# Layer weights loaded into tiles shared with the attention, and the attention's last projections and the layer switch re-placed, in an adaLN transformer block on one core

## The reference, cut to what matters

```python
h = _layernorm(x) * (1 + ca) + sa
x = x + ga * _L0_attn_ref(h, ...)                # 4 heads, all 1024 keys, rms-normed q and k
h = _layernorm(x) * (1 + cb) + sb
x = x + gb * _L0_ffn_ref(h, ...)

def _layer(x, wqkv, qs, ksc, wo, lg, lb, w1, b1, w2, b2):       # twice
    h = shift_token(x)                           # the second half of the features comes from the token before
    q, k, v = jnp.split(h @ wqkv, 3, axis=-1)    # 256 -> 3 * 512
    q, k = rotary_xpos(l2norm(q) * qs, l2norm(k) * ksc)
    x = x + local_attention(q, k, v) @ wo
    h = _layernorm(shift_token(x)) * lg + lb
    a, g = jnp.split(h @ w1 + b1, 2, axis=-1)    # 256 -> 2 * 682
    return x + (a * gelu(g)) @ w2 + b2
```

## Time and profile before

| | us |
|---|---|
| median of 3 runs | 2210.22 (2209.44 to 2210.82) |
| profiled execution | 2207.61 |
| its span | 2205.8 |

### The profile page before, as it was taken

How to read it: one execution, slowest core, us unless ns; L and a number is a source line. 1 busy time by engine, 2 the same in 40 slices (tenths; PEclk the granted TensorE clock), 3 DMA queues, 4 the chain that set the end, 5 groups by cost and what they waited for, 6 DMA issues and landing times.

```text
span 2205.8 us, 36469 instructions
## 1 busy us (share of the span) xinstructions
PE 1865.4 (85%) x12941; PEld 1403.2 (64%) x12941; DVE 1510.0 (68%) x3723; ACT 1186.2 (54%) x2717; POOL 996.6 (45%) x788
## 2 busy tenths in 40 slices
PE   5569999999954799888899888987888999888986
PEld 3444444444433587776777867766776777777776
DVE  3678878877653685766867758584776857768673
ACT  0545545443433656656566565664656566565562
POOL 0325544647463444444444435543545445454451
PEclk7779999999976999999999999998999999999998
DMA  4000010101024000000000002011000000000000
GB/s 141 24 26 27 1 34 11 41 16 51 15 67 134 11 20 17 19 12 24 20 17 21 10 26 68 17 53 32 25 16 29 27 26 25 18 30 26 26 18 22
DMA packets 83407, 68.58 MB, mean 31 GB/s; under 512 B 10853, under 2 KB 79509, under 8 KB 83225
## 3 DMA queue, kind: packets, MB, share of 16 engines
q1 hardware_dynamic: 83224, 66.25, 9.7%
HBM read 45.22 MB, written 16.81 MB: 28 GB/s over the span
## 4 chain that ended last, share of the span: by engine, by line
PE 35%; DVE 18%; issue 6%; ACT 5%; DMA 2%; SPq 1%; POOL 1%; DVEq 0%; ACTq 0%; POOLq 0%
PE bank_O L1201 4%; PE bank_T L1189 3%; PE bank_A L260 3%; PE bank_A L262 3%; PE bank_P L260 3%; PE bank_A L261 3%; ACT l_sm L1337 3%; PE bank_P L261 2%; PE bank_P L262 2%; DVE l_t L1512 2%; PE bank_A L1178 2%; DVE l_sm L1528 2%; DVE l_u_lo L1594 2%; PE bank_T L1168 2%; PE bank_T L260 1%
## 5 line engine op out<-in xcount | busy, mean ns | idle before, releaser
L1737 POOL TENSOR_TENSOR l_sm<-l_sm,l_rinv 128x512 f32<-128x512 f32 (+1 forms) x256 | 250.1, 998 | 366.1 <-DVE l_rinv L1536 365.8
L1725 POOL TENSOR_TENSOR l_t<-l_qk,l_tab 128x512 f32<-128x512 f32 x128 | 170.1, 1350 | 328.8 <-DVE l_ss L1495 328.8
L1337 ACT ACTIVATE l_sm<-l_sm,l_nb 128x256 f32<-128x256 f32 (+1 forms) x512 | 248.1, 486 | 82.0 <-DVE l_nb L1528 81.8
L260 PE MATMUL bank_A<-l_f_hi,l_w_hi 128*114 128x256 f32 (+1 forms) x768 | 220.1, 287 | 3.7 <-DVE l_f_lo L1573 2.7
L262 PE MATMUL bank_A<-l_f_hi,l_w_lo 128*114 128x256 f32 (+1 forms) x768 | 216.0, 281 | 0.0
L261 PE MATMUL bank_A<-l_f_lo,l_w_hi 128*114 128x256 f32 (+1 forms) x768 | 215.8, 281 | 0.0
L1528 DVE CUSTOM_DVE_ANT_0 l_sm<-bank_A,l_mask 128x256 f32<-128x256 f32 (+1 forms) x512 | 177.1, 401 | 52.0 <-PE bank_A L1178 51.5
L1189 PE MATMUL bank_T<-ident,l_sm 128*128 128x128 f32 x960 | 149.1, 290 | 65.7 <-POOL l_sm L1737 34.4
L618 ACT ACTIVATE pr<-ps_S 128x1024 f32<-128x1024 f32 x128 | 130.7, 1023 | 125.4 <-PE ps_S L512 124.6
L1594 DVE TENSOR_TENSOR l_u_lo<-l_up,l_u_hi 114x256 fp32r<-114x256 f32 (+1 forms) x192 | 197.8, 1036 | 0.1
L861 POOL TENSOR_TENSOR acc<-acc,pr 128x1024 f32<-128x1024 f32 x64 | 155.8, 2435 | 51.0 <-ACT pr L618 46.5
(11 more groups left out here) (268 smaller groups left out, 5127.3 us busy)
## 6 DMA issues: line engine op xcount, KB each, us to landing
l_xs<-x_layers SPq DMA_DIRECT2D x64, 128.0 KB, 2.5
x<-in_x SPq DMA_DIRECT2D x8, 512.0 KB, 3.9
base_rows<-x SPq DMA_DIRECT2D x16, 256.0 KB, 2.1
x_layers<-x SPq DMA_DIRECT2D x16, 256.0 KB, 2.1
l_xs<-x_layers SPq DMA_DIRECT2D x64, 64.0 KB, 2.2
x_layers<-l_yb SPq DMA_DIRECT2D x32, 128.0 KB, 1.8
l_base<-base_rows SPq DMA_DIRECT2D x32, 128.0 KB, 3.1
out<-l_yb SPq DMA_DIRECT2D x32, 128.0 KB, 1.7
```

Source lines behind the costliest of these rows:

```text
L260: pe.matmul(out, a_hi, b_hi, start=(start and k == 0), stop=False)
L1337: eng.activation(row, row, ACT.Exp, bias=nb[:, R % SS, e:e + 1], scale=-1.0, accum_out=rsum[:, R % SS, e:e + 1]).then_inc(ex_ready, 1)
L1725: eng.tensor_tensor(dst[:, :, :, lo:lo + H2], src[:, :, :, hi:hi + H2], table[:, :, 1, lo:lo + H2].unsqueeze(2).to_broadcast([P, 2, LH, H2 ...
L1737: eng.tensor_tensor(row, row, rinv[:, R % SS, :].unsqueeze(2).to_broadcast([P, 2, P * windows(n)]), ALU.mult).then_inc(pn_ready, 1)
```

## The change

Five tiles (x, qk, scr, m1, x2) are allocated once for both blocks. The attention uses them as before, and the layers put their own tiles into them (`layer_tiles`). Around this:

1. In the attention, at tick (10, 8), SP issues the loads of the first layer's wqkv, w2 and wo, of the mask, of b2 and of the gains (`load_layers`, 13 DMAs), after waits for the last readers of these tiles. At the layers' start only load(0), load(1), the table, load(2), load(3) and w1 are left to SP.
2. The last two projections go to the banks S0 and S1 instead of X; DVE takes the last reciprocals and `normalise` before the projections' eviction, and `y_split` before the row statistics.
3. DVE modulates the last four row pairs, 12 to 15.
4. SP doesn't wait for the stores at the attention's end; a load of layer 1 waits for the h0 stores of its own sequence, and w1's loads for all stores.
5. In g = -1, first_w2_wo goes from POOL to DVE (k = 4), norms(0) from k = 8 to 6, rotated(0) from 9 to 7, rotated(1) to 9; the table is multiplied in four parts; trig(1) and trig(3) wait until DVE's norms are done; trig(3) goes to round 2 of group 0, and v of units 2 and 3 to its rounds 0 and 2.
6. In group 7, wqkv's pieces go one to a round, at 5 to 10, DVE subtracts them, and the table's parts stand at rounds 8 to 11. In group 8, wo goes to round 4, w1 to 5, 9 and 10, w2 to the slots k = 7, 9 and 11 through other buffers. The waits of later steps for these are narrowed. The gains of layer 2 are loaded in group 1.

The diff, cut to its core:

```diff
+def layer_tiles(share):
+    x, qk, scr, m1, x2 = (share[n] for n in ("x", "qk", "scr", "m1", "x2"))
+    at = {"qk": qk[:, 0:3 * 2 * LH * HD].rearrange("p (i h d) -> p i h d", i=3, h=2 * LH),
+          "pt": qk[:, 3 * 2 * LH * HD:16 * D].rearrange("p (i c n) -> p i c n", i=2, c=4),
+          "sm": x[:, 0:SS * 4 * P].rearrange("p (i e n) -> p i e n", i=SS, e=2),
...
@@ attention_block
         def h0_last(i):
-            return i in (4 * B - 3, 4 * B - 1)
+            return i >= 4 * (B - 1)
...
-                    at = "X"
+                    at = "X" if kind != "w" or i < 4 * B - 2 else f"S{i % 2}0"
...
+                last = R - A_LAG == A_RUNS - 1
+                if last:
+                    inverse(A_UNITS - 1, 0), inverse(A_UNITS - 1, 1)
+                    normalise(A_UNITS - 1)
                 for kind, i in fills(n, j):
                     evict(kind, i)
...
+            def load_layers():
+                t.wait_ge(done["qt"], 4 * A_HALVES)
+                t.wait_ge(done["xt"], 2 * A_HALVES)
+                t.wait_ge(h1_ready, 4 * A_HALVES)
+                t.wait_ge(scr_used, 6 * A_HALVES)
+                at = layer_tiles(share)
+                eng.dma_start(at["raw_q"], io["wqkv"][0].rearrange("(k p) n -> p k n", k=KC)).then_inc(early["wq"], 16)
...
+                load_scales(eng, io, at["scales"], early["tab"], 0)
...
+                if n == A_HALVES + 2 and j == 8:
+                    load_layers()
...
-            for f in range(4):
-                t.wait_ge(base_stored[f], 16 * B)
-                t.wait_ge(h0_stored[f], 16 * B)
@@ layers_block
+        LATE_V = ((2, 2), (3, 2))
-        W_Q = {2: (0, 1), 3: (2, 3), 8: (4, 5)}
-        W_O = {2: (0, 1)}
-        W_1 = {3: (0, 1), 7: (2, 3), 8: (4, 5)}
+        W_Q = {5: (0,), 6: (1,), 7: (2,), 8: (3,), 9: (4,), 10: (5,)}
+        W_O = {4: (0, 1)}
+        W_1 = {5: (0, 1), 9: (2, 3), 10: (4, 5)}
...
-        AT_O, AT_1, AT_2 = pieces[0:2], pieces[2:4] + pieces, pieces[0:2] + pieces[3:4]
+        AT_O, AT_1 = pieces[0:2], pieces[2:4] + pieces
+        AT_2 = [pt[:, i, :, :].rearrange("p c n -> p (c n)") for i in range(2)] + pieces[3:4]
...
@@ PE
+                        elif r in (0, 2):
+                            qkv(*LATE_V[r // 2])
@@ ACT
-                        if g == GL and k == 0:
-                            piece_2(0), piece_2(1), piece_2(2)
+                        if g == GL and k in (7, 9, 11):
+                            piece_2((k - 7) // 2)
@@ DVE
             def layer_norm(q, scale):
                 if q >= (UL - QUAD) // 2:
-                    w.wait_ge(wq_ready, KC + 6)
+                    w.wait_ge(wq_ready, KC + 3)
...
+                        if g == GL - 1:
+                            for i in W_Q.get(r - 1, ()):
+                                piece_q(i)
...
-                    if g == -1 and k == 7:
-                        first_w1()
+                    if g == -1:
+                        if k == 4:
+                            first_w2_wo()
+                        if k == 6:
+                            norms(0)
+                        if k in (7, 9):
+                            rotated(k // 8)
+                        if k == 7:
+                            first_w1()
@@ POOL
+                if n in (1, 3):
+                    w.wait_ge(chain, norms_done[n // 2])
...
-            tables(0)
+            for i in range(4):
+                tables(0, i)
...
+                        if r == 2 and g == 0:
+                            trig(3)
...
-                            for i in W_Q.get(r, ()):
-                                piece_q(i)
-                            if r == 10:
-                                tables(1)
+                            if r >= 8:
+                                tables(1, r - 8)
...
-                    if g == GL and k == 0:
-                        piece_2(0), piece_2(1), piece_2(2)
+                    if g == GL and k in (7, 9, 11):
+                        piece_2((k - 7) // 2)
...
-                    if g == -1 and k == 5:
-                        first_w2_wo()
@@ SP
+                else:
+                    for f in range(4):
+                        w.wait_ge(early["h0"][f], 16 * (b + 1))
...
             load(0), load(1)
-            eng.dma_start(raw_q, io["wqkv"][0].rearrange("(k p) n -> p k n", k=KC)).then_inc(wq_loaded, 16)
-            load(2), load(3)
-            tables(0)
...
+            table(), load(2), load(3)
+            for f in range(4):
+                w.wait_ge(early["base"][f], 16 * B)
+                w.wait_ge(early["h0"][f], 16 * B)
...
                     w.wait_ge(trig_ready, 3 * UL)
-                    tables(1)
+                    table()
                 if g == GL:
                     take_rest()
+                if g == 1:
+                    w.wait_ge(tab_ready, 4)
+                    load_scales(eng, io, scales, tab_loaded, 1)
...
+                if g == GL:
+                    take_2(0)
                 shift(first + 3)
+                if g == GL:
+                    take_2(1), take_2(2)
```

184 lines of the change are left out of this document (98 added, 86 removed).

## The result

| | before | changed |
|---|---|---|
| median of 4 runs, us | 2209.83 (2204.66 to 2210.82) | 2188.27 (2183.93 to 2189.37) |
| profiled execution, us | 2207.61 | 2188.08 |
| its span, us | 2205.8 | 2186.3 |

The ratio is 0.9902, with a 95% interval of 0.9885 to 0.992: 21.6 us faster. The forecast was 2174 in a range of 2160 to 2190. The direction is right and the time lies in the range, but outside the narrower 2163 to 2185 that the prediction gave the forecast itself: 36.5 us were forecast and 60% of them came. The question is where the other 15 went.

The account below looks back on a forecast made before the run. TensorE, busy 85% of the span, was taken as the bound, so only its standstills or half-clock stretches could give time: seam -23, group 7 0, group 8 -13.5, sum -36.5 from 2210.2, forecast 2174 us, range 2160 to 2190.

Parts of the forecast that it names:

- The seam up to the first matmul: From the attention's last projections to the layers' first matmul: earlier projections, modulation, load(0) and weights, -16.0 us.
- ScalarE's wait of 7.78: At the layers' start: ScalarE's wait for w2 and wo goes, -7.8 us.
- part A: The seam, from the attention's last projections to group 0's first probabilities: -23 us, bounds -29 to -18.
- The term of +3.1: At the layers' start: VectorE's three subtractions of w2 and wo, 2.9 us and a bit more beside GpSimd.
- The first rival: Seam and group 7: moved subtractions stand fully behind GpSimd instructions, 2182 us in all, chance 0.12.
- trig(3)'s -5.0: Norms' chain ahead of group 0 freed of trig(3), -5.0 us; trig(3) inside group 0 costs +1.75.
- Group 7: Second layer's wqkv and table loads: the wait for the table offsets the gain, 0 us, bounds -6 to +4.
- Group 8: Second layer's wo, w1 and w2 loads, excess 17.3 us: -13.5 us, bounds -16 to -9.
- the 13.0 go: In group 8, the 13.0 us of excess behind the second residual vanish; 4.3 arise in the rounds before it.
- The prediction's own sign of being wrong: Group 8 keeping more than 9 us of its excess would mean the stop was not w2's.
- the third rival: Layers' start: w1's loads, cast and subtractions or TensorE's low clock give back half of part A, 2188 to 2190, chance 0.03.
- the rival of dearer tile addresses: All 16 groups: shared tiles at other SBUF addresses make operations dearer, kernel slower, 2215 us, chance 0.02.

Follow-up runs that it names:

- e9: Kernel before the change, with only w2's DMAs of both layers cut into 112 rows and the rest, and their wait counts adjusted: 2192.2 us, ratio 0.9928.
- e8: Changed kernel with the early loads undone, the old DMAs back at the layers' start in the old order: one run of 2198.58 us.
- e1: Changed kernel with the second layer's w2 DMAs cut into 112 rows and the rest: 2180.55 us, ratio 0.986.
- e6: Changed kernel with the three subtractions of w2 and wo back on GpSimd, behind trig(0): one run of 2187.8 us.
- e3: Changed kernel with trig(3) back behind trig(2), without the wait for the norms' chain: one run of 2185.54 us.
- e4: Changed kernel with w2's and wo's casts and subtractions moved to the layers' very start, behind the first two units' inputs: 2184.46 us, ratio 0.9872.
- e5: e4 with w1's casts and subtractions also moved behind the fourth unit's input: 2177.44 us, ratio 0.986.
- e11: e10 with trig(3) back behind trig(2), without the wait for the norms' chain: 2164.21 us, ratio 0.9798.
- e10: Changed kernel with e2, e5 and e7 together: 2166.28 us, ratio 0.9806.
- e2: Changed kernel with the table's DMA in group 7 issued ahead of wqkv's last two pieces: 2181.92 us, ratio 0.986.
- e7: e1 with GpSimd's subtractions of w2 in group 8 also put behind trig and the norms' chain: 2178.17 us, ratio 0.9863.

## Why the prediction was right, and where it was not

**The seam up to the first matmul: right.** Forecast -16.0, measured -16.8. Each step came as worked out: the last two projections (the lo part's release 2.3 us earlier where 2 was said), VectorE's eight modulations at 0.69 where the bound was 1.64, load(0) -7.7 where -7.0 was said.

**ScalarE's wait of 7.78, taken as -7.8: mis-sized.** The wait is gone, but no run shows it to be worth 7.8. In e9, which takes the same wait out of the kernel before, the first probabilities come 3.6 us nearer (+95.4 against +99.0). In e8, with the loads late again, the stretch from the first matmul to the first probabilities is 48.6 us against 46.9, although the subtractions in it are 3.8 shorter. The prediction's own bound named this, a wait that mostly covers other work, with -18 for the whole of part A; -16.0 came.

**The term of +3.1 for w2's and wo's subtractions: mis-sized.** They took 6.97 us, 3.8 more than alone. This was the step at which the prediction had the two values next to each other and chose the wrong one: it reasoned that VectorE loses less than GpSimd's own instructions last, "so it is no full stop for the length of one". The rows show full stops: the one of 3.36 (1.22 alone) ends 1.1 behind GpSimd's L1805, which ends at 680.17, and the one of 2.37 ends with GpSimd's L1805 of trig(2), at 708.4, as L89's 2.31 in e1 does with another. The rule of the Trainium skill quoted there (the later of the two waits until the other is through) is what the row of 3.36, with its two SBUF inputs, shows; L89 has one, so the rule as quoted does not cover it. The first rival's mechanism was at work in the seam, though not in group 7, where it had placed the other half of its price.

**The stretch between.** From the first matmul to the first probabilities -8.4 was forecast and -4.6 came. The 3.8 missing are as much as the subtractions took too long, but that this is their cause is not shown: in e6 VectorE is free of them and the first probabilities come at +78.2 all the same. The term of -7.8 is off too, trig(3)'s -5.0 came as -4.0 (e3), and the table is ready 8.6 us behind the first matmul instead of 8.0; how these overlap stays open. What is shown is that the order was worth more than the engine: e4 brings the first probabilities 5.0 us nearer and e5 4.1 more, that one by moving w1's subtractions behind the fourth unit's input.

**trig(3): the gain did not come.** -5.0 for the freed chain and +1.75 inside group 0 were forecast, -3.25 in sum. By e3 the move gave 4.0 and cost 5.6, by e11 against e10 it gave 4.1 and cost 3.7. The failing step is the cover: 3.09 us of GpSimd's idle time were taken as room for 4.84. In group 0's first rounds there is no such room. GpSimd, TensorE and VectorE wait for one another there, and beside VectorE's rotated() trig(3) takes 6.8, not 4.84. TensorE's granted clock between the first probabilities and the first residual is 0.65 with trig(3) there, 0.82 in e3 and 0.79 before. A window of the changed kernel inside that stretch (columns as in the earlier trace rows) has 0.64, largely the lower of the two levels, after TensorE stood between the pairs of probabilities:

```profile
720.00:730.00 10.00, 9.11 (x51) 6.38 (x51) 5.91 (x22) 6.17 (x18) 4.37 (x5) 0.64 0.01 2
```

**Group 7: right.** Forecast 0, measured +0.9. The wait for the table was forecast at 4 to 5 us and measured at 4.60; e2 shows that without it the group takes 93.45 us, and that it was the larger part of what stood in the way. The other 2.2 us over 91.2 were not tried.

**Group 8: half of the forecast.** -13.5 forecast, -6.8 measured, and the two parts came out otherwise than they were read. Of the rounds' 4.3 us, of which the prediction took half a microsecond, 3.0 went. Of the 13.0 behind them, which were all to go, 3.8 went. The failing step is "the 13.0 go": I read VectorE's 11.52 us and SyncE's 8.98 us as what lies *behind* the pieces of w2 and never asked why three DMAs of under 230 KB should stop a queue. The cause moved with the pieces. At k = 9 ScalarE stood for it 9.4 us. Of the missing 6.7 us e1 gives 3.5 back and e7 2.9, together 6.4. The prediction's own sign of being wrong was met here (over 9 us of excess kept: 10.5), but what it would have concluded, that the stop was not w2's, is refuted by e9.

**The number and the third rival.** 2188 us is also what the third rival had (2188 to 2190, chance 0.03), and its mechanism is there: TensorE stands 8.5 us for the fourth unit's input (5.3 before), behind w1's two subtractions of 6.3, and moving them in e5 gives 5.0 at group 0's end. But by that rival all of the loss lay in part A, where 7.0 of the missing 14.9 us lie; 6.7 lie in group 8, of which it says nothing. That its number came is chance, and that the forecast's range holds 2188 it owes to this rival's having been taken into it.

**The rest.** The sum of the clean parts is -16.0 + 0.9 - 6.8 = -21.9 and the medians say -21.6. No other group became longer by more than the scatter, so the rival of dearer tile addresses has nothing for it. The early loads were taken to cost nothing, and no cost shows: the eviction in the attention stands at 633.58 with them and at 633.90 in e8 without.

## What to carry to other kernels

Look at the outermost size of a DMA before looking at its place: one of 113 rows moved here at 23 to 25 GB/s and one of 114 at 141 to 145, against up to 298 once they were cut at 112, and the row or two split off cost a second issue of 0.4 to 0.6 us (0.72 to 1.03 for two in e7, 0.30 to 0.48 for one in the changed kernel). When a wait is removed by moving work, ask what made the work long, for it moves along. Beside a running GpSimd instruction, cost a VectorE operation with two SBUF inputs, or one like L89 and L90, by the time at which that instruction ends, and put chains of small operations where GpSimd is idle. Not every operation pays: the sums of squares (L1543) took their 1.22 us at 704.05 while GpSimd's L1800 ran from 703.50 to 706.04.

## What the runs showed of the hardware

A DMA of 114 rows ran at 141 to 145 GB/s and one of 113 rows at 23 to 25, against up to 298 GB/s when the same rows went in 112 and the rest. With three such DMAs ahead of them two stores took SyncE 8.98 us to issue, and 0.87 once the DMAs were cut (e9). A VectorE operation of 0.18 us lasted 2.31 and one of 1.22 lasted 3.36 beside GpSimd. The same matmul of the layers' start took 0.63 us in one kernel and 0.39 in another with the same code up to there, since TensorE was granted the higher clock earlier. And the attention took between 628.6 and 635.1 us to the same instruction in fourteen profiles; what makes either difference stays open.
